# A selective scan on one Trainium2 core: add and state clip in one saturating add, the fourth group's products in one instruction

## The reference, cut to what matters

```
dA   = exp(clip(dt_t[:, :, None] * A, -20, 0))
dB_u = clip(dt_t[:, :, None] * B_t[:, None, :] * u_t[:, :, None], -10, 10)
h    = clip(h * dA + dB_u, -100, 100)
y    = einsum('bdn,bn->bd', h, C_t)
```

## Time and profile before

| quantity | value |
|---|---|
| time, median of 3 runs | 2228.34 us (2224.9 to 2229.88) |
| the profiled execution's own time | 2224.2 us |
| its span, first to last instruction | 2222.4 us |
| busy PE / PEld | 1748.5 us (79%) / 1113.5 us (50%) |
| busy DVE | 1544.9 us (70%) |
| busy ACT | 978.4 us (44%) |
| busy POOL | 442.1 us (20%) |
| scan recurrence in the span | about 1334 to 1806 us |

### The profile page before, as it was taken

The page is one execution under the profiler, slowest core; times in us unless marked ns, Lnnn a source line. Parts: engine busy times, 40 slices in busy tenths (PEclk is TensorE's granted clock), DMA queues, the critical chain, the costliest instruction groups (busy, mean ns, idle before and its releaser), DMA issues. The chain is left out here.

```text
span 2222.4 us, 37721 instructions
## 1 busy us (share of the span) xinstructions
PE 1748.5 (79%) x11568; PEld 1113.5 (50%) x11568; DVE 1544.9 (70%) x3313; ACT 978.4 (44%) x2622; POOL 442.1 (20%) x466
## 2 busy tenths in 40 slices
PE   5999999999996799688895845667666643399998
PEld 3666666666663355455554734445444433244443
DVE  3666666666664566566674448999999995477776
ACT  2555555555553233233331358878878720011110
POOL 0111111111110000000000106665565644000000
PEclk9999999999998799899897977888888876699999
DMA  2110010110101900000461000000000000100000
GB/s 77 29 28 19 28 28 19 28 28 19 28 19 31 289 0 0 21 0 0 154 193 59 0 0 1 1 0 1 0 1 0 0 10 0 43 1 11 10 5 14
DMA packets 69411, 66.57 MB, mean 30 GB/s; under 512 B 5753, under 2 KB 66896, under 8 KB 69328
## 3 DMA queue, kind: packets, MB, share of 16 engines
q1 hardware_dynamic: 66516, 64.00, 9.4%
q10 hardware_dynamic: 2812, 1.66, 0.3%
HBM read 61.45 MB, written 4.19 MB: 30 GB/s over the span
## 5 line engine op out<-in xcount | busy, mean ns | idle before, releaser
L1844 PE MATMUL ss_y_ps<-ss_h,ss_diag 128*128 128x256 f32 x1024 | 307.5, 461 | 190.9 <-DVE ss_h L1805 153.2
L1844 PEld LDWEIGHTS ss_y_ps<-ss_h,ss_diag 128*128 128x128 f32 x1024 | 230.3, 233 | 267.8 <-DVE ss_h L1805 184.4
L418 ACT ACTIVATE x_probs<-x_s_ps,x_neg_max 128x257 f32<-128x257 f32 x512 | 238.8, 472 | 250.8 <-DVE x_neg_max L489 250.8
L489 DVE TENSOR_REDUCE x_neg_max<-x_s_ps 128x2 f32<-128x514 f32 x256 | 174.2, 681 | 179.0 <-PE x_s_ps L288 179.0
L1734 ACT ACTIVATE ss_decay<-sc_dt,sc_a 128x256 f32 (+1 forms) x496 | 206.5, 462 | 90.2 <-DVE ss_come L1799 87.4
L496 DVE COPY x_pT<-x_pT_ps 128x512 f32<-128x512 f32 x256 | 175.5, 686 | 42.6 <-PE x_pT_ps L298 38.4
L285 PE MATMUL x_s_ps<-x_kT,x_qblk 32*128 32x257 f32 x1024 | 182.5, 433 | 0.0
L298 PE MATMUL x_pT_ps<-all_ident,x_probs 128*128 128x128 f32 x1024 | 169.9, 289 | 0.6 <-ACT x_probs L418 0.5
L1744 ACT ACTIVATE ss_come<-ss_dtu,sc_xd 128x256 f32<-128x256 f32 x384 | 161.8, 494 | 6.6 <-POOL ss_dtu L1692 6.6
L1788 DVE SCALAR_TENSOR_TENSOR ss_decay<-ss_decay,ss_h 128x1024 f32<-128x1024 f32 x124 | 151.2, 1219 | 7.4 <-ACT ss_decay L1734 7.4
L1799 DVE SCALAR_TENSOR_TENSOR ss_come<-ss_come,ss_decay 128x1024 f32<-128x1024 f32 x124 | 149.3, 1204 | 0.0
(11 more groups left out here) (358 smaller groups left out, 3318.9 us busy)
## 6 DMA issues: line engine op xcount, KB each, us to landing
x_ctx_t<-ctxT SPq DMA_DIRECT2D x48, 514.0 KB, 3.8
kept_ctx_t<-ctxT SPq DMA_DIRECT2D x16, 514.0 KB, 8.3
kept_ctx_n<-ctx SPq DMA_DIRECT2D x16, 512.0 KB, 8.6
x_ctx_n<-ctx SPq DMA_DIRECT2D x16, 512.0 KB, 3.9
all_x<-x SPq DMA_DIRECT2D x4, 512.0 KB, 7.1
x_mid<-all_x SPq DMA_DIRECT2D x32, 64.0 KB, 3.8
all_x<-x_mid SPq DMA_DIRECT2D x4, 512.0 KB, 7.5
out<-all_x SPq DMA_DIRECT2D x8, 256.0 KB, 2.1
```

The costliest lines, as they stand in the source:

```text
L418: ins = nc.scalar.activation(probs[p][:, n, :], s_ps[u % 2][:, j, 0:S2], ACT.Exp, bias=neg_max[p][:, n:n + 1], accum_out=sums[p][:, n:n + 1])
L489: vec.tensor_reduce(neg_max[p][:, 2 * u:2 * u + 2], s_ps[u % 2][:, :, 0:S2], AX.X, ALU.max, negate=True).then_inc(max_sb, 1)
L1844: ins = nc.tensor.matmul(y_ps[p][:, 0:DI], diag[q][:, m, :], h[q][:, m, :], start=(q == 0 and m == 0), stop=(q == NQ - 1 and m == NH - 1))
```

## The change

The change is confined to `scan_states`. VectorE's `add` and `clip` of a group become `state`, one `TENSOR_ADD_SAT` instruction: h = max(min(come + decay, 100), -100), with `come` in SBUF, `decay` in PSUM and `h` in SBUF. The lower clip at -10, which `add` had held, is in GpSimd's `bound` for groups 0 to 2, where it stood already; group 3 now gets a `bound` as well. `bound_last`, four products of 256 elements with a pointer scalar, becomes `mine`, one `tensor_tensor` of 1024 elements with both operands broadcast (dt·u over the four states, the four weights over the channels), and it moves from the end of a position to behind the first `state` of it. ScalarE's `decays` wait for the finished state (`h_sb`) in place of the sum (`sum_sb`).

```diff
-NQP = NQ - 1
+OWN = (0, 0, 0, 4)
+BY_ACT = [q for q in range(NQ) if OWN[q] < NH]
+BY_DVE = [q for q in range(NQ) if OWN[q] > 0]
...
             def bound(t, k, q):
-                pool.wait_ge(raw_sb, t * NQP + q + 1)
+                if q in BY_ACT:
+                    pool.wait_ge(raw_sb, t * len(BY_ACT) + BY_ACT.index(q) + 1)
+                if q in BY_DVE:
+                    pool.wait_ge(mine_sb, t * len(BY_DVE) + BY_DVE.index(q) + 1)
...
             def position(t, k, first=False, last=False):
                 for q in range(NQ):
-                    if q < NQP and not last:
+                    if not last:
                         bound(t + 1, k + 1, q)
                     diagonals(t, q)
...
                 if not (isinstance(n, int) and n < RING):
-                    act.wait_ge(sum_sb, n - RING + 1)
+                    act.wait_ge(h_sb, n + NQ - RING + 1)
...
-            def bound_last(t, k):
+            def mine(t, k, q):
 
                 dve.wait_ge(dtu_sb, t + 1)
                 if not (isinstance(t, int) and t < 2):
-                    dve.wait_ge(h_sb, (t - 2) * NQ + L + 1)
-                for m in range(NH):
-                    s = 1 + L * NH + m
-                    ins = vec.tensor_scalar(come[L][k % 2][:, m, :], dtu[k % 2][:, :], xd[:, t, s:s + 1], 10.0, ALU.mult, ALU.min)
-                ins.then_inc(last_sb, 1)
+                    dve.wait_ge(h_sb, (t - 2) * NQ + q + 1)
+                m = OWN[q]
+                weight = xd[:, t, 1 + q * NH:1 + q * NH + m]
+                vec.tensor_tensor(come[q][k % 2][:, 0:m, :], dtu[k % 2][:, :].unsqueeze(1).to_broadcast([P, m, DI]),
+                                  weight.unsqueeze(2).to_broadcast([P, m, DI]), ALU.mult).then_inc(mine_sb, 1)
...
-            def add(t, k, q):
+            def state(t, k, q):
                 n = (t - 1) * NQ + q
                 dve.wait_ge(kept_psum, n + 1)
-                if q < L:
-                    dve.wait_ge(bound_sb, (t - 1) * NQP + q + 1)
-                else:
-                    dve.wait_ge(last_sb, t + 1)
-                c = come[q][k % 2][:, :, :].rearrange("p m d -> p (m d)")
-                vec.scalar_tensor_tensor(c, c, -10.0, decay[ring(k, q)][:, :], ALU.max, ALU.add).then_inc(sum_sb, 1)
-
-            def clip(t, k, q):
-                n = (t - 1) * NQ + q
-                dve.wait_ge(sum_sb, n + 1)
+                dve.wait_ge(bound_sb, n + 1)
                 dve.wait_ge(y_psum, n + 1)
-                vec.tensor_scalar(h[q][:, :, :], come[q][k % 2][:, :, :], 100.0, -100.0, ALU.min, ALU.max).then_inc(h_sb, 1)
+                dve.sem_inc(waited_dve, 1)
+                vec._custom_dve(bass.dve_ops.TENSOR_ADD_SAT, out=h[q][:, :, :].rearrange("p m d -> p (m d)"),
+                                in0=come[q][k % 2][:, :, :].rearrange("p m d -> p (m d)"),
+                                in1=decay[ring(k, q)][:, :], s0=100.0, s1=-100.0).then_inc(h_sb, 1)
 
             def position(t, k, first=False, last=False):
                 for q in range(NQ):
                     kept(t, k, q)
                     if q >= 1:
-                        add(t, k, q - 1)
+                        state(t, k, q - 1)
                     elif not first:
-                        add(t - 1, k - 1, L)
-                    if q >= 2:
-                        clip(t, k, q - 2)
-                    elif not first:
-                        clip(t - 1, k - 1, q + 2)
-                if not last:
-                    bound_last(t + 1, k + 1)
+                        state(t - 1, k - 1, L)
+                    if not last and q < len(BY_DVE):
+                        mine(t + 1, k + 1, BY_DVE[q])
```

More of the change, by code:

```diff
@@ L1665, in scan_states @@
         y_ps = [ps(f"y_ps{p}", [P, BANK]) for p in range(2)]
-        dtu_sb, raw_sb, bound_sb, last_sb, diag_sb = (sem(n) for n in ("dtu_sb", "raw_sb", "bound_sb", "last_sb", "diag_sb"))
-        decay_psum, kept_psum, sum_sb, h_sb = (sem(n) for n in ("decay_psum", "kept_psum", "sum_sb", "h_sb"))
+        dtu_sb, raw_sb, mine_sb, bound_sb, diag_sb = (sem(n) for n in ("dtu_sb", "raw_sb", "mine_sb", "bound_sb", "diag_sb"))
+        decay_psum, kept_psum, h_sb = (sem(n) for n in ("decay_psum", "kept_psum", "h_sb"))
         y_psum, y_sb = sem("y_psum"), sem("y_sb")
-        waited_act, waited_pool = sem("waited_act"), sem("waited_pool")
+        waited_act, waited_pool, waited_dve = sem("waited_act"), sem("waited_pool"), sem("waited_dve")
         block = ctx.enter_context(nc.Block())
@@ L1689, in dt_u @@
                 if not (isinstance(t, int) and t < 2):
-                    pool.wait_ge(raw_sb, (t - 1) * NQP)
-                    pool.wait_ge(last_sb, t - 1)
+                    pool.wait_ge(raw_sb, (t - 1) * len(BY_ACT))
+                    pool.wait_ge(mine_sb, (t - 1) * len(BY_DVE))
                 nc.gpsimd.tensor_tensor(dtu[k % 2][:, :], dt[:, t, :], uz[:, t, 0:DI], ALU.mult).then_inc(dtu_sb, 1)
             def bound(t, k, q):
-                pool.wait_ge(raw_sb, t * NQP + q + 1)
+                if q in BY_ACT:
+                    pool.wait_ge(raw_sb, t * len(BY_ACT) + BY_ACT.index(q) + 1)
+                if q in BY_DVE:
+                    pool.wait_ge(mine_sb, t * len(BY_DVE) + BY_DVE.index(q) + 1)
                 pool.sem_inc(waited_pool, 1)
@@ L1716, in _ @@
             for q in range(NQ):
-                if q < NQP:
-                    bound(1, 1, q)
+                bound(1, 1, q)
                 diagonals(0, q)
@@ L1741, in raw @@
                 act.sem_inc(waited_act, 1)
-                for m in range(NH):
+                for m in range(OWN[q], NH):
                     s = 1 + q * NH + m
@@ L1754, in position @@
                     decays(t, k, q)
-                    if q < NQP and not last:
+                    if q in BY_ACT and not last:
                         raw(t + 1, k + 1, q)
@@ L1760, in _ @@
             for t in range(2):
-                for q in range(NQP):
+                for q in BY_ACT:
                     raw(t, t, q)
@@ L1810, in position @@
                     if q >= 1:
-                        add(t, k, q - 1)
+                        state(t, k, q - 1)
                     elif not first:
-                        add(t - 1, k - 1, L)
-                    if q >= 2:
-                        clip(t, k, q - 2)
-                    elif not first:
-                        clip(t - 1, k - 1, q + 2)
-                if not last:
-                    bound_last(t + 1, k + 1)
-            bound_last(0, 0)
+                        state(t - 1, k - 1, L)
+                    if not last and q < len(BY_DVE):
+                        mine(t + 1, k + 1, BY_DVE[q])
+            for q in BY_DVE:
+                mine(0, 0, q)
             for q in range(NQ):
[L1824 to L1827, removed]
+                if q in BY_ACT:
+                    dve.wait_ge(raw_sb, BY_ACT.index(q) + 1)
+                if q in BY_DVE:
+                    dve.wait_ge(mine_sb, BY_DVE.index(q) + 1)
                 vec.tensor_scalar(h[q][:, :, :], come[q][0][:, :, :], 10.0, -10.0, ALU.min, ALU.max).then_inc(h_sb, 1)
-            bound_last(1, 1)
+            for q in BY_DVE:
+                mine(1, 1, q)
             positions(dve, position)
[L1831 to L1834, removed]
+            state(T - 1, T - 1, L)
         @block.tensor
```

## The result

The changed kernel takes 2126.31 us (median of 4 runs, 2125.18 to 2127.76). Its ratio to the kernel before is 0.9545, with a 95% interval of 0.9526 to 0.9564. The forecast was 2132 in a range of 2121 to 2168. The profiled execution has a span of 2123.6 us against 2222.4. One more run of the kernel before took 2456.12 us, over 10% above its other three, and the ratio leaves it out.

The account below looks back on a forecast made before the run. VectorE bound the scan; ScalarE would next, at 11.65 us a position against 14.69. Saving 91.1 us over thirty positions and 4.5 in the last took 2224.2 to 2128.6, or 2132 us as median; range 2121 to 2168.

Parts of the forecast that it names:

- VectorE bound, then ScalarE bound: In the scan, VectorE bounds before; after, its 10.3 to 11.35 us a position falls below ScalarE's 11.56, which becomes the bound.
- The saturating add at 1.12: VectorE's four `state` instructions: each was taken at 1.12 us, like `add`, with bounds of 1.08 and 2.16.
- a dearer one: Rival at VectorE's `state`: saturating add costs 1.72 us, as add and clip together; about 2183 us, chance 0.06.
- two passes: Rival at the four `state` instructions: two passes over the data, 2.16 us each; 2237 us, slower than before, chance 0.05.
- `mine` at 1.26: VectorE's broadcast product for group 3: 1.14 us plus 0.12 for waiting on the `state` directly in front.
- the credit beside it: VectorE's removed `bound_last`, four products: 2.69 us a position taken as saved.
- The lock: VectorE and GpSimd exclude each other on SBUF: `mine` was charged 0.5 us a position, bounds 0 and 1.04.
- The rival of a bad rhythm: VectorE and GpSimd lock into a worse rhythm around `mine`: period 12.3 to 12.4 us, about 2154 us, chance 0.15.
- ScalarE's sum of 11.56, with 0.1 on top: ScalarE's own work in a position, 11.56 us, plus 0.1 for loop ends and small waits: period 11.65.
- The last position: End of the recurrence, at VectorE's pace: 13.1 us after the change against 17.55 before, 4.5 saved.
- GpSimd's fourth bound: GpSimd's added `bound` for group 3: its sum becomes 9.7 us, 10.8 with one held, under 11.56; thin cover.
- TensorE: Rival: TensorE's matmuls become the bound at its lower clock, 14.1 us a position; 2207 us, chance 0.03.

Follow-up runs that it names:

- e4: Changed kernel with nine of ScalarE's twelve raw products of a position left out from position 2 on: 2097.48 us, ratio 0.9409.
- e3: Changed kernel with a stock two-input add in place of the saturating add, the ±100 clip of the state left out: 2128.30 us, ratio 0.9553.
- e1: Changed kernel with group 3's products again four small instructions at the end of a position, without a clip; saturating add kept: 2126.93 us, ratio 0.9546.
- e2: Changed kernel with the saturating add split into add and clip again, the broadcast product at the end of a position: 2201.92 us, ratio 0.9881.
- e7: Changed kernel with keep_y early, group 3's product as four small ones in front, one group 2 product moved from ScalarE to VectorE: 2185.69 us.
- e10: Changed kernel with two group 2 products moved from ScalarE to VectorE, all six small products at the end of a position: 2153.68 us, ratio 0.9670.
- e5: Changed kernel with keep_y issued after the exponentials of group 0 in place of those of group 3: 2129.24 us, ratio 0.9559.
- e12: Changed kernel, one group 2 product moved to VectorE; five small products end a position, group 3's first, GpSimd's bounds awaiting the last: 2130.21 us.
- e11: Changed kernel with keep_y early and one group 2 product moved from ScalarE to VectorE, products in two-input broadcast form: 2136.63 us, ratio 0.9597.
- e6: Changed kernel with the broadcast product written as four small products at the same place, the front of a position: 2126.49 us, ratio 0.9550.

## Why the prediction was right, and where it was off

**VectorE bound, then ScalarE bound.** Right, and e4 shows the second part as an effect: less work on ScalarE alone gives 29 us, 28 of them in the recurrence.

**The saturating add at 1.12.** Right: 1.13 to the next start, 1210 ns, the same as a stock add of the same shapes (e3). The cases of a dearer one and of two passes are out. The Trainium skill ("Vector Engine (DVE) Microarchitecture Reference", section 3.4) says that programs written for the engine's pipeline that hold values in its delay cells run at the built-in rate, with a figure for two int32 inputs. The two rows agree: this instruction, with one input in PSUM, reads 1210 ns as the stock add does.

**`mine` at 1.26.** Right in size (0.15 of waiting and 1.14). But the credit beside it was misread. I took 2.69 for the cost of the four products removed. e1 shows 1.14 for them and the time unchanged. The gain that I booked to this half of the change is not there beside the other half: the saturating add alone brings everything, and the product alone 25 us (e2). The total came out right because ScalarE's sum stands above VectorE's in either form, so the size of this term never reached the result. A forecast of the saturating add alone would have failed by it, as my expectation of e1 did, which put VectorE at 11.7 and above ScalarE.

**The lock.** I put 0.5 a position on `mine`. Its mean duration is 1.30 in the changed kernel between 1400 and 1690 us, against 1.23 undisturbed, so the charge is under 0.1: two of the 25 there waited and read 2.11. The order favours it: where it starts with a GpSimd instruction it mostly wins, and GpSimd's `diagonals` then reads 2.09 in place of 1.04. The rival of a bad rhythm did not come up in this kernel, but a rhythm of that kind is real, and e7 to e10 show it with small products: up to 2.2 us a position. The Trainium skill's rule of the exclusive pair ("SBUF — State Buffer", "Who interferes with whom") agrees with every product row above, from 1.14 with GpSimd idle to 3.71 with it busy. That `kept` never exceeds 1.22 was misread by 0.01 (the 1.23 in the earlier trace rows); nothing hangs on it.

**ScalarE's sum of 11.56, with 0.1 on top.** Measured 11.45 over the thirty positions, a shade under the 11.5 to 11.8 that I named as the sign. The term mis-sized is keep_y: I used its duration of 0.36, while the next start comes 0.26 later (1586.40 to 1586.66). With that the sum is 11.46, and it closes. The charge of 0.1 for waits was not needed either. Together they are 0.2 × 30 = 6.1 us more gain than forecast.

**The last position.** Forecast 13.1, measured 14.5. The nine instructions of VectorE take 10.3 as forecast, but I counted 2.5 us for TensorE's last products. In the changed kernel a position's first unit waits for keep_y, which ScalarE issues last, so all 32 records of position 31 run behind it in one burst of 7.14, which ends 3.7 us after the last state. With keep_y early (e5) this stretch is 13.4. The late burst costs most of the 1.4 us missed here.

**The rest of the difference.** The first `kept` comes 0.2 us later and the last stretch of the program is 1.3 us longer, within what the stretches outside the recurrence vary by. In the profiles the sum is 95.6 + 6.1 - 1.4 - 0.2 - 1.3 = 98.8 us, as measured. The forecast misses by 5.7 us, not by 3.2, because I carried over the 4.1 us between the profiled execution and the median of the kernel before; in the changed kernel that gap is 0.9.

**GpSimd's fourth bound.** Free as forecast: GpSimd is busy 86 of 100 us and ScalarE never waits for it in the middle window. That the cover is thin, e12 shows: when GpSimd idles 2.4 us for a product, dt_u comes late.

**TensorE.** Never the bound: it is busy for 71.16 of 100 us in the middle. The granted clock there is 0.90, where it was 0.83 before the change. In e4 it is 1.00 without a gain being traced to it.

## What to carry to other kernels

Before booking the removal of an instruction at its duration, ask whether that duration is work: a row that reads 2.7 us for four products can be 1.1 of work and 1.6 of waiting for the other engine, and in e2 part of the waits moved to other instructions of VectorE, the clips. Where VectorE and GpSimd share the work, one wide instruction is safer than four narrow ones (e11 against e7), and instructions whose result the partner must wait for run undisturbed (e1, e12). Here VectorE and ScalarE were within 10% of each other, and moving work between them brought out other limits (the lock in e7 to e10, GpSimd's order in e12) before it brought the gain that the sums promised.

## What the runs showed of the hardware that was not expected

- Four products of 256 elements on VectorE take 1.14 us with GpSimd idle (e1), 1.98 to 2.10 beside one GpSimd instruction (e6), 2.77 and 3.71 beside several (the earlier trace rows and e7): VectorE's next product waits until the GpSimd instruction that came in between has ended. In e7 the four end between 0.14 and 0.15 us after the GpSimd instruction beside each.
- A custom three-step VectorE instruction, 1024 elements with one input in PSUM, and a stock one-step add of the same shapes both read 1210 ns.
- A ScalarE copy of 256 elements out of PSUM reads 0.36 us, and the next instruction starts after 0.26; four exponentials read 1.65 to 1.69 with 1.60 to the next start.
